# Query and key biases and a layer norm's scale folded into projection weights, and six gelus in one visit of ScalarE

## The reference

```python
for i in range(8):                      # LAYERS
    residual = x
    Q  = elu(x @ Wq[i] + bq[i]) + 1     # 16 heads of 64: 1024 channels
    Kf = elu(x @ Wk[i] + bk[i]) + 1
    V  = x @ Wv[i] + bv[i]
    KV, sumK = sum_s(Kf * V), sum_s(Kf) # per channel, over the tokens of an image
    att = Q * KV / (Q * sumK + 1e-6)
    y = gelu(att @ Wo[i] + bo[i])
    x = layer_norm(y + residual) * ln1_s[i] + ln1_b[i]
    h = gelu(x @ W1[i] + b1[i])         # 512 wide
    h = gelu(h @ W2[i] + b2[i])
    x = layer_norm(h + x) * ln2_s[i] + ln2_b[i]
```

## Time and profile before

| | us |
|---|---|
| median of 3 runs | 3271.7 (3268.28 to 3273.61) |
| profiled execution | 3271.77, its span 3269.6 |
| PE busy | 2953.8 (90%) |
| DVE busy | 2672.6 (82%) |
| ACT busy | 2419.0 (74%) |
| POOL busy | 853.8 (26%) |

### The profile page before, as it was taken

How to read it: one execution, slowest core, us unless ns; L and a number is a source line. 1 busy time by engine, 2 the same in 40 slices (tenths; PEclk the granted TensorE clock), 3 DMA queues, 4 the chain that set the end, 5 groups by cost and what they waited for, 6 DMA issues and landing times. The chain is left out here.

```text
span 3269.6 us, 50808 instructions
## 1 busy us (share of the span) xinstructions
PE 2953.8 (90%) x14297; PEld 1961.7 (60%) x14297; DVE 2672.6 (82%) x10489; ACT 2419.0 (74%) x4498; POOL 853.8 (26%) x1032
## 2 busy tenths in 40 slices
PE   6999998364799999999999999999999999999868
PEld 5777776253466666665666666566666666655545
DVE  4656565864689999998999999899999899989967
ACT  5888886122588888887888888788888878877743
POOL 2444443266111111112111111211111121122326
PEclk9999999587899999999999999999999999999988
DMA  1000000323100000000000000000000000000001
GB/s 56 1 0 0 0 0 1 111 36 64 46 1 1 22 12 1 20 7 8 1 26 8 1 20 7 8 1 27 7 1 20 7 7 1 20 7 7 1 1 39
DMA packets 32201, 49.49 MB, mean 15 GB/s; under 512 B 5395, under 2 KB 21859, under 8 KB 31718
## 3 DMA queue, kind: packets, MB, share of 16 engines
q1 hardware_dynamic: 26342, 42.64, 3.9%
q0 software_dynamic: 5632, 4.20, 1.0%
HBM read 38.31 MB, written 8.51 MB: 14 GB/s over the span
## 5 line engine op out<-in xcount | busy, mean ns | idle before, releaser
L2070 DVE TENSOR_SCALAR t_feat_q<-t_recip,t_neg_mean 128x256 f32<-128x256 f32 x1024 | 410.0, 462 | 111.9 <-ACT t_recip L1887 109.2
L1624 PE MATMUL t_o_ps<-t_feat_q,t_wo 128*128 128x512 f32 x1008 | 469.1, 598 | 7.7 <-issue 4.1
L1879 ACT ACTIVATE t_recip<-t_feat_q,t_z_scale 128x256 f32<-128x256 f32 x1024 | 434.8, 499 | 4.4 <-DVE t_feat_q L2070 3.7
L1865 ACT ACTIVATE t_exp_k<-t_k_ps 128x1024 f32<-128x1024 f32 x256 | 259.7, 1015 | 230.4 <-PE t_k_ps L1598 230.4
L2033 DVE CUSTOM_DVE_ANT_0 t_junk<-t_v_ps,t_feat_k 128x256 f32<-128x256 f32 x1024 | 390.1, 418 | 12.3 <-PE t_v_ps L1598 12.0
L2290 POOL TENSOR_TENSOR t_var_eps<-t_moments,t_ln_eps 128x4 f32<-128x4 f32 x128 | 67.5, 527 | 1224.1 <-DVE t_moments L2081 1224.1
L2023 DVE SCALAR_TENSOR_TENSOR t_feat_k<-t_exp_k,t_k_ps 128x256 f32<-128x256 f32 x1024 | 368.9, 416 | 15.7 <-ACT t_exp_k L1865 15.7
L1869 ACT ACTIVATE t_exp_q<-t_q_ps 128x1024 f32<-128x1024 f32 x256 | 261.5, 1022 | 86.5 <-PE t_q_ps L1598 85.5
L2059 DVE SCALAR_TENSOR_TENSOR t_feat_q<-t_exp_q,t_q_ps 128x1024 f32<-128x1024 f32 x256 | 312.7, 1221 | 8.8
L1624 PEld LDWEIGHTS t_o_ps<-t_feat_q,t_wo 128*128 128x128 f32 x1008 | 191.9, 191 | 178.8 <-issue 158.4
L243 POOL TENSOR_TENSOR a_probs<-a_probs,a_inv 128x256 f32<-128x256 f32 (+1 forms) x256 | 209.2, 839 | 275.6 <-DVE a_inv L340 275.6
(11 more groups left out here) (441 smaller groups left out, 7223.6 us busy)
## 6 DMA issues: line engine op xcount, KB each, us to landing
t_raw_w<-in_wk SPq DMA_DIRECT2D x8, 512.0 KB, 3.7
t_raw_w<-in_wq SPq DMA_DIRECT2D x8, 512.0 KB, 4.6
t_raw_w<-in_wv SPq DMA_DIRECT2D x8, 512.0 KB, 5.5
t_raw_o<-in_wo SPq DMA_DIRECT2D x8, 512.0 KB, 3.7
t_raw<-in_w SPq DMA_DIRECT2D x16, 256.0 KB, 2.7
x<-in_x SPq DMA_DIRECT2D x4, 512.0 KB, 7.0
tokens_dram<-r_hn SPq DMA_DIRECT2D x8, 256.0 KB, 2.3
e_w_raw<-in_fc_w SPq DMA_DIRECT2D x4, 512.0 KB, 3.9
```

Source lines behind the costliest of these rows:

```text
L1624: last = pe.matmul(out[:], wo[:, chunk, :], feat_q[:, s, chunk, :], start=(chunk == 0), stop=(chunk == NC - 1), skip_group_check=True)
L1865: act.activation(exp_k[:], k_ps[:], ACT.Exp, bias=-1.0).then_inc(c["k_exp"], 1)
L1879: last = act.activation(recip[:, q % 2, k * UNIT + n * SEQ:k * UNIT + (n + 1) * SEQ], feat_q[:, s, chunk, cols], ACT.Ln, bias=1.0, scale=z ...
L2070: last = dve.tensor_scalar(feat_q[:, s, chunk, cols], recip[:, q % 2, k * UNIT + n * SEQ:k * UNIT + (n + 1) * SEQ], -1.0, neg_mean[:, s, n ...
```

## The change

The second layer norm's scale and shift are no longer applied when a unit leaves a layer: `state_t` gets the norm plus 1. Since the features of a norm sum to 0, the sum of such a column is 128, and a constant divided by 128 can be added to every row of the weight: for layers 1 to 7 the projections use a folded weight, `diag(s) W + (1/128) 1 ((b - s) W + bias)`. TensorE makes it in six pieces a layer, in steps 1 to 6, into the bank of the output projection (`fold_piece`); ScalarE copies out the high part and VectorE the low part (`split_piece`). The matrix for it is made once a layer (`make_fold`). The bias matmuls stay in layer 0 only. The residual needs the true state, so ScalarE restores it in place, once a unit (`restore_x`), and VectorE's addition waits for that. On ScalarE gelus 2 and 3 join the first visit, and on TensorE products 2 and 3 of the feed-forward come earlier. The hardware loop begins at step 8 instead of 4, again with three turns. In the experts' phase `AHEAD` is 4, the splitting of the biases comes later, and two steps of VectorE come earlier.

```diff
-        AHEAD = 3
+        AHEAD = 4
...
             dve.wait_ge(c["small_in"], 32)
             mark(0)
-            split_biases()
...
             split_weights(1)
             read_slots(3)
+            split_rows(1)
+            gate_rows(0)
             mark(4)
-            split_rows(1)
             read_slots(4)
-            gate_rows(0)
...
             gate_rows(2)
+            split_biases()
             sum_gates()
...
+        def folds(at):
+            return 1 <= at % PER <= 6 and at < UNITS - PER
+        def piece_of(at):
+            return (at % PER - 1) // 2, (at % PER - 1) % 2
... TensorE
+            def fold_piece(t, at):
+                kind, half = piece_of(at)
+                layer = layer_of(t) + 1
+                pe.wait_ge(c["raw_w_in"], 48 * layer + 49)
+                pe.wait_ge(c["fold_ready"], layer + 1)
+                if at >= 2:
+                    pe.wait_ge(c["y1_ready"], t - 2 + 2)
+                if kind < 2:
+                    pe.wait_ge(c["raw_b_in"], 64 * layer + 65)
+                    pe.matmul(o_ps[:], bias_pick[:, 2 * kind + half, :], raw_b[:].rearrange("p q c -> p (q c)"), start=True, stop=False,
+                              skip_group_check=True)
+                pe.matmul(o_ps[:].rearrange("p (q c) -> p q c", c=P), fold_m[:], halves(raw_w[:, kind, :])[:, :, half, :],
+                          start=(kind == 2), stop=True, skip_group_check=True).then_inc(c["w_folded"], 1)
...
+                biased = at < PER
                 if A:
-                    pe.wait_ge(c["b3_ready"], layer_of(t) + 2)
-                    biases(t, w, 0)
+                    if biased:
+                        biases(t, 0)
                     pe.wait_ge(c["x_split"], t + 2)
-                    queries(t, s, w, 0)
-                    keys(t, s, w, 0)
+                    queries(t, s, w, 0, biased)
+                    keys(t, s, w, 0, biased)
...
                     first_feed_forward(t - 3, 1)
-                if A:
-                    biases(t, w, 1)
-                    values(t, s, w, 0, 0)
-                    keys(t, s, w, 1)
-                    queries(t, s, w, 1)
-                if Dn:
                     first_feed_forward(t - 3, 2)
                 if A:
-                    values(t, s, w, 0, 1)
+                    if biased:
+                        biases(t, 1)
+                    values(t, s, w, 0, 0)
                 if Dn:
                     first_feed_forward(t - 3, 3)
+                if A:
+                    if folds(at):
+                        fold_piece(t, at)
+                    keys(t, s, w, 1, biased)
+                    queries(t, s, w, 1, biased)
+                if A:
+                    values(t, s, w, 0, 1)
+                if folds(at):
+                    pe.wait_ge(c["w_ready"], 6 * layer_of(t) + 6 + at % PER + 1)
                 if B:
                     project(t - 1, r, 0)
... ScalarE
                 if Dn:
                     first_gelu(t - 3, 1)
+                    first_gelu(t - 3, 2)
+                    first_gelu(t - 3, 3)
                 if A or B:
                     act.preload_act_table_set("natural_log_exp_and_others")
                 if B:
                     exp_z(t - 1, 0)
+                if folds(at):
+                    split_piece(t, at)
                 if A:
                     exp_keys(t, 1)
                     exp_queries(t, 1)
-                if Dn:
-                    first_gelu(t - 3, 2)
-                    first_gelu(t - 3, 3)
-                if A or B:
-                    act.preload_act_table_set("natural_log_exp_and_others")
...
                     exp_queries(t, 3)
+                    if at >= PER:
+                        restore_x(t)
+                    if at % PER == 0 and at < UNITS - PER:
+                        make_fold(t)
                 if B:
                     log_z(t - 1, r, 3)
... VectorE
                 if B:
                     attention(t - 1, r, 0)
+                if folds(at):
+                    split_piece(t, at)
                 if A:
                     feature_k(t, s, 1)
...
                 if C:
+                    dve.wait_ge(c["restored"], t - 2 + 2)
                     dve.wait_ge(c["y1_ready"], t - 2 + 2)
```

More of the change, by code:

```diff
@@ L1296, in _ @@
             pool.memset(g["t_pool_carrier"][:], 0.0).then_inc(c["zeroed"], 1)
+            pool.memset(g["t_bias_pick"][:], 0.0).then_inc(c["pick_zeroed"], 1)
+            pool.wait_ge(c["pick_zeroed"], 1)
+            for k in range(4):
+                pool.memset(g["t_bias_pick"][32 * k:32 * k + 3, k, :], 1.0 / D).then_inc(c["pick_made"], 1)
+            pool.wait_ge(c["pick_made"], 4)
             def add(n):
@@ L1503, in half_of, with halves @@
             return at // PER % 2
[L1505 to L1511, removed]
+        def folds(at):
+            return 1 <= at % PER <= 6 and at < UNITS - PER
+        def piece_of(at):
+            return (at % PER - 1) // 2, (at % PER - 1) % 2
+        def halves(row):
+            return row.rearrange("p (q h c) -> p q h c", h=2, c=P)
         def active(at, lag):
@@ L1582, in _, with biases @@
             ident = g["ident"][:]
-            def biases(t, half_of_w, q):
+            def biases(t, q):
                 pe.wait_ge(c["k_ready"], 4 * t + q + 1)
@@ L1590, in biases @@
                         rows = slice(32 * (2 * kind + half), 32 * (2 * kind + half) + 3)
-                        pe.matmul(out[:, half * UNIT:(half + 1) * UNIT], b3[rows, half_of_w, q, :], ones_b[rows, :],
+                        pe.matmul(out[:, half * UNIT:(half + 1) * UNIT], b3[rows, 0, q, :], ones_b[rows, :],
                                   start=True, stop=False, skip_group_check=True)
@@ L1702, in step @@
                     values(t, s, w, 1, 0)
-                    biases(t, w, 2)
-                    queries(t, s, w, 2)
+                    if biased:
+                        biases(t, 2)
+                    queries(t, s, w, 2, biased)
                 if C:
@@ L1710, in step @@
                 if A:
-                    keys(t, s, w, 2)
+                    keys(t, s, w, 2, biased)
                 if E:
@@ L1727, in step @@
                     values(t, s, w, 2, 0)
-                    biases(t, w, 3)
-                    keys(t, s, w, 3)
-                    queries(t, s, w, 3)
+                    if biased:
+                        biases(t, 3)
+                    keys(t, s, w, 3, biased)
+                    queries(t, s, w, 3, biased)
                     values(t, s, w, 2, 1)
@@ L1856, in modulate, with split_piece, make_fold, restore_x @@
                 act.activation(g["f_h_hi"][n], g["state_t"][:, n, :], ACT.Copy).then_inc(f["h_hi_ready"], 1)
-            def split_weights(layer, w, k):
-                act.wait_ge(c["raw_w_in"], 48 * layer + 49)
-                act.activation(w_hi[:, w, k, :], raw_w[:, k, :], ACT.Copy).then_inc(c["w_hi_ready"], 1)
+            def split_piece(t, at):
+                kind, half = piece_of(at)
+                act.wait_ge(c["w_folded"], 6 * layer_of(t) + at % PER + 1)
+                act.activation(halves(w_hi[:, 1 - half_of(at), kind, :])[:, :, half, :], o_ps[:].rearrange("p (q c) -> p q c", c=P), ACT.Copy)\
+                   .then_inc(c["w_hi_ready"], 1)
+            def make_fold(t):
+                layer = layer_in_range(t)
+                act.wait_ge(c["w_ready"], 6 * layer_of(t) + 7)
+                act.activation(fold_m[:], g["ident"][:], ACT.Identity, bias=fold[:, bass.ds(layer, 1), 1], scale=params[:, bass.ds(layer, 1), 8])\
+                   .then_inc(c["fold_ready"], 1)
+            def restore_x(t):
+                layer = layer_in_range(t - PER)
+                place = g["state_t"][:, bass.ds(place_of(t), 1), :]
+                act.wait_ge(c["x_split"], t + 2)
+                act.activation(place, place, ACT.Identity, bias=fold[:, bass.ds(layer, 1), 0], scale=params[:, bass.ds(layer, 1), 8])\
+                   .then_inc(c["restored"], 1)
             def exp_keys(t, q):
@@ L2005, in _, with split_piece @@
         def _(dve):
[L2006 to L2014, removed]
+            def split_piece(t, at):
+                kind, half = piece_of(at)
+                out, hi = (halves(w[:, 1 - half_of(at), kind, :])[:, :, half, :] for w in (w_lo, w_hi))
+                dve.wait_ge(c["w_hi_ready"], 6 * layer_of(t) + 6 + at % PER + 1)
+                dve.tensor_tensor(out, o_ps[:].rearrange("p (q c) -> p q c", c=P), hi.bitcast(F32), ALU.subtract).then_inc(c["w_ready"], 1)
             def feature_k(t, s, q):
```

65 lines of the change are left out of this document (35 added, 30 removed), and 1 row of the table names.

## The result

The changed kernel takes 3344.97 us (median of 4 runs, 3341.49 to 3349.65), the kernel before 3271.24 (3268.28 to 3273.61): ratio 1.0226, 95% interval 1.0213 to 1.0239. It is slower by 73.7 us. The forecast was 3356, with 3280 to 3395 as its range. The profiled execution took 3341.49 us (span 3339.7), so the two traces differ by 69.7 us.

A forecast was written before the change was run, and what follows sets the result against it. The bound was taken to be a loop through VectorE, TensorE and ScalarE, 35.17 us a unit. Terms 73 + 4 + 27 - 19 = +85 on the profiled 3271.8 gave about 3356 us, range 3280 to 3395.

The forecast's parts named there:

- The loop: VectorE's run from attention chunk 0 to the last query feature, next queries, ScalarE's work through chunk 0's reciprocal: 35.17 us.
- Unit, +1.2, 61 times, +73: Gelus in one visit: chunk 0's reciprocal waits for TensorE's later fourth feed-forward product; unit 36.4 us, +1.2 in 61 units.
- the other three groups: TensorE's bias matmuls outside chunk 0: removing them gains 0, as they stand where TensorE waits for VectorE.
- Fold, 0.65 in 42 units, +27: VectorE's subtraction for the folded weights, between attention chunk 0 and the keys' feature: 0.65 us in 42 units, +27.
- What goes, -19: Bias copy and weight split no longer done: 2.75 us less in each of 7 layers, -19.
- Restored state, 0: ScalarE's one activation a unit to restore the state is hidden, cost 0; without cover 0.3 in 56 units, +17.
- Biases kept in layer 0, +4: The first 8 units keep bias matmuls; two groups lie on the longer path, 0.85 us in 5 units, +4.
- Ahead of the layers, 0: Experts' phase: a fourth gather before the first addition and later bias splitting, taken as 0, ends -11 and +11.
- 1: ScalarE's or TensorE's own time decides, so faster: 3201 us if TensorE, about 3162 if ScalarE; chance 0.09.
- 2: The two moved gelus are hidden as VectorE's run shrinks, nearly no change: +12, 3284 us; chance 0.11.
- 3: TensorE idles more and its clock falls, much slower: +220 on top, about 3575 us; chance 0.05 together with 4.
- 4: The change saves no table loads, as restore or fold would add two of 1.28 us; chance 0.05 together with 3.

The follow-up runs named there:

- e2: The kernel before with all six gelus in one visit and the product order that goes with it, biases by matmuls, no fold: 3412.68 us, ratio 1.0421.
- e10: The kernel before with GpSimd's low part of the next unit's input and its weight copies held until after attention chunk 1: 3255.17 us, ratio 0.9964.
- e1: The changed kernel, folded weights kept, with gelus 2 and 3 and products 2 and 3 put back behind chunk 0's reciprocal (two visits): 3247.05 us, ratio 0.9915.
- e6: The changed kernel with GpSimd's copies of the two feed-forward weights held until after VectorE's attention chunk 1: 3335.9 us, ratio 1.0202.
- e7: The changed kernel without the restoring of the state on ScalarE, one activation a unit left out: 3342.72 us, ratio 1.022.
- e9: The changed kernel with two visits, GpSimd's low input part and weight copies after attention chunk 1, state restored before keys 3's exponential: 3218.93 us, ratio 0.9842.

## Why the prediction was right, and where it was off

The loop was the right bound, the path by TensorE the right one of the two, and the sign follows. By its terms:

- *Unit, +1.2, 61 times, +73.* Measured +0.72, +44. The term is oversized in one place: VectorE's run was put at 21.8 and is 21.24. The step that failed is "the other three groups ... I cost them at 0". e2 has them and runs 21.90 with a 0.19 wait for keys 3 and 1.99 in attention chunk 1, where the changed kernel has none and 1.64. Taking away the bias groups of chunks 2 and 3 shortened VectorE's run through keys 3, the path of which e10 gives the lengths. The other members hold: 10.90 + 0.53 against 11.1 + 0.2, 0.70, 1.30, 1.06, 0.10.
- *Fold, 0.65 in 42 units, +27.* Measured 36.44 - 35.88 = 0.56, +24. In e1 a fold unit is 0.6 to 1.1 over the plain 33.98.
- *What goes, -19.* Here two things were taken for one. 2.75 us a layer were read off as bias copy and weight split; 1.2 of them are GpSimd's weight copies beside attention chunk 1, which the change keeps (e10: 36.4 becomes 35.13, bias copy still in place). What went is 1.55 x 7 = -11, and the copies grew to 1.5 a unit (e6), +2.
- *Restored state, 0.* e7: -2 us, 0 within the error. *Fold matrix, 0*: the unit in which it is made is 0.3 longer, +2 (without the restoring, e7, it is not).
- *Biases kept in layer 0, +4.* Layer 0 grew by 14 us (from 274.5 to 288.6) where layers 1, 3 and 5 grew by 8.3 to 8.4: +6. Three of its units take 37.60, 1.15 over a fold unit of the later layers, where 0.85 had been put, with the groups of chunks 2 and 3 at 0 again; the one in which the feed-forward's gelus first join the visit takes 38.76 (33.95 before). What of that is the bias groups was not separated.
- *Ahead of the layers, 0*: the first split of the layers starts at 823.7 against 825.6, -2.

Measured so: 44 + 24 + 2 + 2 - 11 + 6 - 2 = +65, some 5 short of the 69.7 between the traces; the units at the two back edges of the hardware loop (40.51 and 39.80 after) are 1.5 of them, the rest was not taken apart. Against +85 that is 34 too much on the unit, the fold and the moves ahead, and 19 too little on all else: the mechanism was right, but that the total came within 11 us of the median is in part luck.

The rivals: 1 is out (e1: with more loads it is faster; engines less busy and the unit longer). 2 is out, though the reserve it named did shrink (1.99 to 1.64). 3 is out: the granted clock is 0.99 in the layer, though TensorE now idles 1.10 us before the first output product (1969.58); at the back edge of the earlier trace rows it was 0.57 from 2094 to 2098. 4 is out: two loads a unit, as the change says.

The rule weighed: the Trainium skill (ScalarE: Activation LUTs, Table sets: the hidden batching unit) says to group calls by table set. Here grouping two visits into one cost 102 us (e1 against the changed kernel, by their ratios) although it saves two loads of 1.28 us a unit: ScalarE waits 2.85 us before the exponential of keys 3 (1985.00 in the trace after) and has that time to give, while the calls that were pulled forward stand in front of the one activation that VectorE needs.

## What to carry to other kernels

Before work is grouped to save set-up cost, find the loop that sets the period, and look on which side of its hand-over the moved work lands: behind the hand-over it was free, ahead of it every 0.1 us counts. When a term that is now hidden is taken away, look for a second path of nearly the same length; here folding the biases away gained 64 us net in one order of the gelus and 28 in the other. And an excess read off as a difference of unit lengths belongs to everything that happens in that unit, on every engine.

## What the runs showed of the hardware

VectorE's attention step (SBUF to SBUF, 128x256, four times) takes 1.14 us alone. It took 1.64 (after) and 1.99 (before) beside one GpSimd instruction of 1.3 that ran along with it for 0.70 and 1.05, 3.12 beside the end of that instruction, a copy and a second subtraction, and 3.90 in the last layer. Its normalising step, which reads PSUM, took 1.35 to 1.37 throughout the layers, also where GpSimd ran beside it for 0.8 us or more (e9, e10). The Trainium skill (SBUF — State Buffer, SBUF: two separate sides) calls the port pair that VectorE and GpSimd share an exclusive lock, held for a whole instruction. Those times fit that: the step is longer by 0.50 and 0.85, somewhat less than the time both ran. e6 and e9 got the time back with waits on GpSimd and no less work: by the ratios 8 us of 3345 with the one wait of e6, and 24 us from e1 to e9, which has two such waits and one moved activation; their shares were not separated.
